# Queries by one f32 matmul instead of three bf16 parts, one-hots in f32 with two chunks interleaved, and a ring of three for the block sums

## The reference

```python
q = (X @ Wq)[src]                 # 64 wide
k = (X @ Wk)[dst]
e = jnp.tanh(q + k)
scores = e @ Wphi
exp_scores = jnp.exp(scores - jnp.max(scores))
denom = jax.ops.segment_sum(exp_scores, src, num_segments=N)
alpha = exp_scores / (denom[src] + 1e-09)
msg = alpha[:, None] * ((X @ Wy_w + Wy_b)[dst] + e @ We)
out = jax.ops.segment_sum(msg, src, num_segments=N)
x = layernorm(x + out)
```

## Time and profile before

| | |
|---|---|
| median of three runs | 5431.57 us (5428.85 to 5432.63) |
| the profiled execution | 5425.74 us, of which the span of its instructions is 5424.0 us |
| PE matmul | 3511.2 us busy, 65% of the span |
| PE weight load | 2746.3 us, 51% |
| DVE | 4216.0 us, 78% |
| ACT | 3684.6 us, 68% |
| POOL | 3537.4 us, 65% |
| mean granted clock of TensorE | 0.779 of full |

### The profile page before, as it was taken

One profiled execution on the slowest core, in us unless ns is written; L12 is line 12 of the kernel. 1 busy time (PEld: TensorE's weight loads), 2 busy tenths in 40 slices (PEclk: granted clock), 3 DMA queues, 4 the chain that ended last, 5 costly groups with the idle time before them and its releaser, 6 DMA issues. The chain is left out here.

```text
span 5424.0 us, 91419 instructions
## 1 busy us (share of the span) xinstructions
PE 3511.2 (65%) x19333; PEld 2746.3 (51%) x19333; DVE 4216.0 (78%) x9852; ACT 3684.6 (68%) x14197; POOL 3537.4 (65%) x3559
## 2 busy tenths in 40 slices
PE   7799999955555665555655555556655555556557
PEld 7566566644444444444444444444544444444446
DVE  7699999977777777777777777777777777777776
ACT  3699999966666666666666666666666666666667
POOL 1034434357777777777777777777777777777771
PEclk9899999977777767777777777776677777777778
DMA  3200000023333333333333333333333333333334
GB/s 89 73 5 5 5 5 5 5 71 106 106 106 102 106 106 107 103 106 106 106 103 107 106 105 103 106 107 105 104 106 107 106 103 106 106 105 102 106 98 110
DMA packets 284190, 478.09 MB, mean 88 GB/s; under 512 B 94226, under 2 KB 203892, under 8 KB 283385
## 3 DMA queue, kind: packets, MB, share of 16 engines
q0 software_dynamic: 165184, 324.30, 23.0%
q1 hardware_dynamic: 100662, 142.95, 7.8%
q10 hardware_dynamic: 17794, 4.91, 0.4%
HBM read 456.43 MB, written 20.60 MB: 88 GB/s over the span
## 5 line engine op out<-in xcount | busy, mean ns | idle before, releaser
L1112 POOL DMA_INDIRECT gathered<-table,dst_rows x3276 | 3151.2, 962 | 1008.9 <-issue 992.1
L1146 PE MATMUL bank<-gathered,weighted_onehots 128*128 128x193 f32 x6592 | 1913.4, 455 | 1458.6 <-DVE block_sums L1235 1450.4
L1146 PEld LDWEIGHTS bank<-gathered,weighted_onehots 128*128 128x128 f32 x6592 | 1582.1, 267 | 1661.9 <-issue 997.4
L1235 DVE TENSOR_TENSOR block_sums<-block_sums,bank 128x193 f32 x3296 | 1166.8, 354 | 541.1 <-issue 166.0
L1198 DVE TENSOR_REDUCE gathered<-bank 128x128 f32<-128x384 f32 x1648 | 840.5, 552 | 446.0 <-DMA gathered<-table,dst_rows 435.0
L1157 ACT ACTIVATE gathered<-gathered 128x256 f32<-128x256 f32 x824 | 346.5, 421 | 1202.8 <-DVE gathered L1202 1202.8
L1167 ACT ACTIVATE weighted_onehots<-src_distances,score_less_shift 128x128 f32<-128x128 bf16 x3296 | 1052.4, 390 | 26.9
L1175 ACT ACTIVATE src_distances<-row_to,src_in_block 128x128 bf16<-128x128 f32 x3296 | 1039.6, 386 | 0.0
L822 ACT ACTIVATE places_past_far<-bank,stat 128x98 bf16<-128x98 f32 x2727 | 889.2, 1237 | 18.8 <-PE bank L847 18.8
L822 ACT ACTIVATION_READ_ACCUMULATOR places_past_far<-bank,stat 128x1 f32 x2727 | 887.9, 1097 | 0.0
L1135 PE MATMUL bank<-q_parts,src_onehots_T 128*128 x3296 | 614.7, 317 | 272.6 <-DVE gathered L1202 231.2
(11 more groups left out here) (190 smaller groups left out, 2272.5 us busy)
## 6 DMA issues: line engine op xcount, KB each, us to landing
src_in_block_rows<-src_in_block_list SPq DMA_DIRECT2D x206, 512.0 KB
gathered<-table,dst_rows POOLq DMA_INDIRECT x3276
gathered<-table SPq DMA_DIRECT2D x2560, 0.8 KB
table<-in_x SPq DMA_DIRECT2D x4, 1562.5 KB
x_in<-in_x SPq DMA_DIRECT2D x24, 256.0 KB, 2.9
x_again<-in_x SPq DMA_DIRECT2D x48, 128.0 KB, 2.3
out<-out_rows SPq DMA_DIRECT2D x48, 128.0 KB, 1.9
sorted_list<-sorted_groups,unit_destinations POOLq DMA_INDIRECT x248
```

The lines of the kernel that those rows point to most:

```text
L1112: e.indirect_dma_start(slot[:, r, j, 0:ROW], None, table, bass.IndirectOffsetOnAxis(ap=gidx[:, t:t + 1].bitcast(u32), axis=0)).then_inc(ga ...
L1146: made = e.matmul(SM[q % 2 * 2 + j // 2][:, o:o + SUMS], ohw[:, q % 3, j, :], slot[:, r, j, A:SLOT], start=True, stop=True)
L1235: e.tensor_tensor(sums[:, bass.ds(b, SUMS)], sums[:, bass.ds(b, SUMS)], SM[q % 2 * 2 + j // 2][:, o:o + SUMS], ALU.add).then_inc(accumulat ...
```

## The change

The queries are kept as one f32 array. The query matmul of a tile is one f32 matmul with 64 columns, and the four tiles of a step go to one bank. The one-hots for it are written in f32, into an array in which the two chunks alternate element by element, so that both the writing VectorE instruction and the weight load step over every second f32 element. The two reductions of line 1198 go; the addition of the key reads the queries from PSUM. The banks that come free make a ring of three steps for the products, and the sums are added one step later (s-5). The plan loses the operations that made the parts, and two steps of its loop.

```diff
-        q3 = sb(ctx, "q_parts", [PARTS, NB * 3 * A], bf16)
+        q32 = sb(ctx, "queries", [PARTS, NB * A], f32)
...
-        XSTEPS = NQ + XR + 2
+        XSTEPS = NQ + XR
...
-                    e.activation(q3v[:, b0:b0 + n, 0, :], kst[:, k % XR, 0:n, A:2 * A], ACT.Copy).then_inc(q0_made, 1)
-                k = i - (XR + 1)
-                if 0 <= k < NQ:
-                    b0, n, _ = q_split(k)
-                    e.wait_ge(rest_made, k + 1)
-                    e.activation(q3v[:, b0:b0 + n, 1, :], rest[:, k % 2, 0:n, :], ACT.Copy).then_inc(q1_made, 1)
+                    e.activation(q32v[:, b0:b0 + n, :], kst[:, k % XR, 0:n, A:2 * A], ACT.Copy).then_inc(queries_kept, 1)
...
-                    e.tensor_tensor(rest[:, k % 2, 0:n, :], kst[:, k % XR, 0:n, A:2 * A], q3v[:, b0:b0 + n, 0, :],
-                                    ALU.subtract).then_inc(rest_made, 1)
...
-                    e.tensor_tensor(q3v[:, b0:b0 + n, 2, :], rest[:, k % 2, 0:n, :], q3v[:, b0:b0 + n, 1, :], ALU.subtract).then_inc(q2_made, 1)
...
-        ohT = sb(lists, "src_onehots_T", [PARTS, 2, CHUNK * PARTS], bf16)
+        ohT = sb(lists, "src_onehots_T", [PARTS, CHUNK * PARTS, 2], f32)
...
-        QK, SM = [[bank[0], bank[1]], [bank[2], bank[3]]], [bank[4], bank[5], bank[6], bank[7]]
+        QK, SM = [bank[0], bank[1]], [[bank[2 + 2 * i], bank[3 + 2 * i]] for i in range(3)]
...
-        TAIL = 5
+        TAIL = 6
...
-                        made = e.matmul(QK[q % 2][j // 2][:, j % 2 * 3 * A:(j % 2 + 1) * 3 * A], ohT[:, c % 2, o:o + PARTS], q3[:, bass.ds(b, 3 * A)],
+                        made = e.matmul(QK[q % 2][:, j * A:(j + 1) * A], ohT[:, o:o + PARTS, c % 2], q32[:, bass.ds(b, A)],
                                         start=True, stop=True)
...
-                    if q >= 2:
-                        e.wait_ge(accumulated, (q - 1) * QUAD)
+                    if q >= 3:
+                        e.wait_ge(accumulated, (q - 2) * QUAD)
...
-                        made = e.matmul(SM[q % 2 * 2 + j // 2][:, o:o + SUMS], ohw[:, q % 3, j, :], slot[:, r, j, A:SLOT], start=True, stop=True)
+                        made = e.matmul(SM[q % 3][j // 2][:, o:o + SUMS], ohw[:, q % 3, j, :], slot[:, r, j, A:SLOT], start=True, stop=True)
...
-            e.tensor_scalar(ohT[:, c % 2, :], lob[:, c % LOB, :], part0[:, :], None, ALU.is_equal).then_inc(onehots_T_made, 1)
+            e.tensor_scalar(ohT[:, :, c % 2], lob[:, c % LOB, :], part0[:, :], None, ALU.is_equal).then_inc(onehots_T_made, 1)
...
-                    for h in range(2):
-                        made = e.tensor_reduce(slot[:, r, 2 * h:2 * h + 2, ROW:ROW + A], QK[q % 2][h][:, 0:6 * A].rearrange("p (j s f) -> p j f s", s=3, f=A),
-                                               AX.X, ALU.add)
-                    made.then_inc(query_summed, 1)
-                    e.wait_ge(query_summed, q + 1)
-                    e.tensor_tensor(slot[:, r, :, ROW:ROW + A], slot[:, r, :, ROW:ROW + A], slot[:, r, :, 0:A], ALU.add).then_inc(added_qk, 1)
+                    e.tensor_tensor(slot[:, r, :, ROW:ROW + A], QK[q % 2][:, 0:QUAD * A].rearrange("p (j f) -> p j f", f=A),
+                                    slot[:, r, :, 0:A], ALU.add).then_inc(added_qk, 1)
...
-                q = step - 4
+                q = step - 5
...
-                        e.tensor_tensor(sums[:, bass.ds(b, SUMS)], sums[:, bass.ds(b, SUMS)], SM[q % 2 * 2 + j // 2][:, o:o + SUMS],
+                        e.tensor_tensor(sums[:, bass.ds(b, SUMS)], sums[:, bass.ds(b, SUMS)], SM[q % 3][j // 2][:, o:o + SUMS],
                                         ALU.add).then_inc(accumulated, 1)
```

More of the change, by code:

```diff
@@ L110, in gnn_program @@
         used = sb(ctx, "tiles_used", [1, 1], i32)
-        q3 = sb(ctx, "q_parts", [PARTS, NB * 3 * A], bf16)
+        q32 = sb(ctx, "queries", [PARTS, NB * A], f32)
         bmap = sb(ctx, "tile_blocks", [PARTS, 2, MAPC], i32)
-        q3v = q3[:, :].rearrange("p (b s f) -> p b s f", s=3, f=A)
+        q32v = q32[:, :].rearrange("p (b f) -> p b f", f=A)
         fences = {k: sem(f"fence_{k}") for k in ENGINES}
@@ L164, in gnn_program @@
         x_padded, x_turned, xT_made, kq_made, kst_made = sem("x_padded"), sem("x_turned"), sem("xT_made"), sem("kq_made"), sem("kst_made")
-        q0_made, rest_made, q1_made, q2_made = sem("q0_made"), sem("rest_made"), sem("q1_made"), sem("q2_made")
+        queries_kept = sem("queries_kept")
         hots_made, tiles_counted, tiles_out = sem("hots_made"), sem("tiles_counted"), sem("tiles_out")
@@ L415, in gnn_program @@
         kst = sb(plan, "k_and_q", [PARTS, XR, GB, 2 * A], f32)
-        rest = sb(plan, "q_rest", [PARTS, 2, GB, A], f32)
         tot_row = sb(plan, "block_tiles_int", [PARTS, NB], i32)
@@ L489, in scalar_plan @@
                         e.wait_ge(k_stored[k % XR], x_loads(k - XR))
-                        e.wait_ge(rest_made, k - XR + 1)
-                        e.wait_ge(q0_made, k - XR + 1)
+                        e.wait_ge(queries_kept, k - XR + 1)
                     e.activation(kst[:, k % XR, 0:n, :], kq, ACT.Copy).then_inc(kst_made, 1)
@@ L642, in vector_plan @@
             line.after()
-            line.did(e.tensor_scalar(bmap[:, 0, :], bmf[:, :], float(3 * A), None, ALU.mult))
+            line.did(e.tensor_scalar(bmap[:, 0, :], bmf[:, :], float(A), None, ALU.mult))
             line.did(e.tensor_scalar(bmap[:, 1, :], bmf[:, :], float(SUMS), None, ALU.mult))
@@ L1008, in gnn_program @@
         distances_made, onehots_T_made = sem("src_distances_made"), sem("src_onehots_T_made")
-        query_summed = sem("query_summed")
         queried, added_qk, tanh_made = sem("queried"), sem("added_qk"), sem("tanh_made")
@@ L1016, in gnn_program @@
         leave = {k: sem(f"pass_next_{k}") for k in ENGINES if k != "sync"}
-        pass_sems = [*gathered, *rows_by_sync, *lows_loaded, sums_cleared, distances_made, onehots_T_made, query_summed, queried, added_qk, tanh_made,
+        pass_sems = [*gathered, *rows_by_sync, *lows_loaded, sums_cleared, distances_made, onehots_T_made, queried, added_qk, tanh_made,
                      times_phi, scored, scores_shifted, weighted, totalled, accumulated, row_max, core_max, shift_made, *steps_over.values()]
-        QK, SM = [[bank[0], bank[1]], [bank[2], bank[3]]], [bank[4], bank[5], bank[6], bank[7]]
+        QK, SM = [bank[0], bank[1]], [[bank[2 + 2 * i], bank[3 + 2 * i]] for i in range(3)]
         CLEAR = NB * SUMS * 4 // 9
@@ L1133, in tensor_steps @@
                         o = t % CHUNK * PARTS
-                        b = e.snap(regs[t % CHUNK], min_val=0, max_val=(NB - 1) * 3 * A)
-                        made = e.matmul(QK[q % 2][j // 2][:, j % 2 * 3 * A:(j % 2 + 1) * 3 * A], ohT[:, c % 2, o:o + PARTS], q3[:, bass.ds(b, 3 * A)],
+                        b = e.snap(regs[t % CHUNK], min_val=0, max_val=(NB - 1) * A)
+                        made = e.matmul(QK[q % 2][:, j * A:(j + 1) * A], ohT[:, o:o + PARTS, c % 2], q32[:, bass.ds(b, A)],
                                         start=True, stop=True)
```

## The result

The changed kernel takes 5529.05 us (median of four runs, 5526.56 to 5529.73), the kernel before on the same chip 5430.73 us: a ratio of 1.0176, interval 1.016 to 1.0192. It is slower by 1.8%. The forecast was 5537, with 5500 to 5590 for its own case and 5375 to 5590 with the fast rival.

A forecast was written before the change was run, and what follows sets the result against it. GpSimd's gathers were taken to bound the kernel. Terms +127 - 14 - 8 = +105 us on the profiled 5425.74 gave 5531, and 5.8 us for the median made 5537 us, +1.9%; range 5375 to 5590.

The forecast's parts named there:

- its own case: Main part: f32 one-hots at two numbers a cycle still exclude gathers; 5537 us, chance 0.64.
- the fast rival: One-hots' strided store runs at one number a cycle and leaves gathers alone; 5385 us, chance 0.27.
- GpSimd is the bound: Main part: GpSimd's gathers fill it, 3151.2 us busy plus 992.1 us issue, of 4150 us.
- Line 1182 keeps excluding gathers: Main part, one-hots: writing f32 takes 1.29 us and still shuts out GpSimd's gathers.
- The stall: Gathers beside the one-hots lengthen by 0.74 us a chunk, 152 us, 25 there before: +127 us.
- the formulas: Gather lengthening from one-hots' duration L and start s: s + L + 0.12 - 0.95 below s = 0.45, another form above.
- the shift of 0.2: One-hots start about 0.2 us later into a gather; 0.77 us average lengthening by the formulas.
- Addition from PSUM: Key addition reads one operand from PSUM, so fewer gathers are held: -14 us (0 to -23).
- Plan: Plan before the main part: removed copies and two last steps save time, -8 us (0 to -12).
- Query matmul: TensorE, main part: f32 queries take 1.0 to 2.1 us a step, fitting beside the products, so 0.
- The second rival: TensorE becomes the bound with queries and products at 5.3 us a step; 5643 us, chance 0.03.
- the clock argument: TensorE staying at the lower clock when over 90% busy is unlikely; the sort, 92% busy, has 1.00.

The follow-up runs named there:

- last experiment: Changed kernel with tensor_scalar and PSUM-operand one-hots alternating by 36 chunks, ring of two, GpSimd clearing an array each step; 6471.9 us, kernel before 5437.09.
- light gathers: Gathers fetch 64 numbers instead of 192, in the changed kernel, the version with partition number in PSUM, and the kernel before: 6159.15, 6149.05, 6186.31 us.

## Why the prediction was right

*GpSimd is the bound.* Held, before and after, by the waits. The last experiment shows it by a difference in time (25.1 us) that is the difference in the gathers' own duration (25.2 us), though the two kinds of block also differ in VectorE's work and in TensorE's clock.

*Line 1182 keeps excluding gathers when it writes f32.* Held. Of the two ends that I had for the unknown store, two numbers a cycle (1.29 us) came (1.283), and the exclusion with it. The dense layout makes no difference, so the row of line 589 was the near one and that of line 1367 the far one.

*The stall: 0.74 us a chunk, +127 us.* Measured 0.750 and +128. It rests on the phase. I had the one-hots follow the addition of the key by about 1.36 us and they do by 1.33, and most then begin 0.25 to 0.42 us into a gather. Put to the phases as they lie in the changed kernel, with L = 1.283, the formulas give 0.75, so they hold for the longer instruction too. The phases themselves were not shifted one by one: 183 of the 206 are between 0.20 and 0.45, where the shift of 0.2 would have put 128. The average hardly depends on that (0.77 by the shift), and that 0.74 came within 0.01 is in part luck, as my own trials went from 0.65 to 0.88.

*Addition from PSUM, -14 us.* Measured -17. Gathers over 1.0 us away from the one-hots fell from 130 to 38. What is left is the 9 us forecast; what there was is 26 us by the split above, where the prediction had 22.6, hence 17 for 14. That the rest comes from the multiplication by phi is shown by the version with phi in PSUM, where it goes.

*Plan, -8 us.* The destinations are made at 208.17 for 220.26, 12.1 us earlier; 9.5 of it is left at the first gather.

*Query matmul, 0.* Held: 1207.3 us over 824 steps is 1.47 us a step (1.0 to 2.1 forecast), products and queries together 3.76 us of the 5.17 that a step takes, and GpSimd waited for TensorE 1.8 us. The second rival is out. By its wait, that is, and not by the clock argument that I had against it: another run has a stretch of the plan with TensorE 92% busy and a granted clock of 0.50 (last section), so the row of the sort did not carry it.

*VectorE's time, ring of three, tail.* VectorE's saving went into waits; the sums' wait for `totalled` fell from 28.9 to 1.2 us, hidden; the tail is 1.0 us longer (within 1.5).

The terms came to +128 - 17 - 9.5 + 1.0 = +102.5 against the 103.1 of the spans, and against +105 forecast. The 5537 lies 8 us over the 5529: 2 by the terms, and 5.8 that I had added because the profiled execution of the kernel before lay under its median; after the change it lies on it (5529.14).

*The fast rival* (0.27) needed the exclusion to go with the strided f32 store. It did not; but an instruction of the same output that leaves the port alone exists (2.28 us), and its gathers have the 953 ns that this rival wanted. Its time as a whole kernel on a chip of the first kind was not measured. From the rows: 3276 times 996 less 953 ns is 141 us under the span of 5527.1, an estimate of 5386 us, 38 under the span before. It assumes that nothing else becomes the bound, as in the blocks of this form in the last experiment.

## What to carry to other kernels

When an engine that issues transfers is the bound, work removed from another engine is worth little by itself (here VectorE gave up 741 us, and the time rose), and what that engine's remaining instructions do to the issuer can be worth more. Look for the few long instances of the bounding instruction (mean against median), find what lies beside each, and work the new duration through the phases as they lie. A cheaper instruction that takes the shared port can cost more than one almost twice as long that does not.

## What had not been expected

The hold of a gather goes by the placement of operands as sharply as shown: 2.28 us with one operand in PSUM, surplus 0.01 us; the same with both in SBUF, 1.98 us.

Chips differ in when gathers land: the addition of the key, which waits for it, starts 2.8 us after the last gather's start on one kind and about 20 on the other, with the same 0.946 us of the instruction, and the kernel before takes 5431 or about 6160 us. Only bytes were tried, and they are not the reason (264 or 478 MB, 6150 us); the cause stays open. On these chips the loss of 1.8% does not appear: versions of the changed kernel with the same long gathers have ratios of 0.9955 to 0.9972. With light gathers, the first gather starts at 1150.1 after the change and 1181.0 in the kernel before, 30.9 us apart, while first to last start differ by 6.2 us (4883.2 and 4889.3). So there the early part is what is left to see, and nearly all of the 30.9 us is there when the destinations are made (208.7 and 239.5; on the first chip 208.2 and 220.3). The traces show what goes with its being more than the 12.1 us of the first chip. The same 20 us of the plan (start:end, us, busy of PE, PEld, DVE, ACT and POOL with their counts, granted clock, DMA share, GB/s), in the kernel before on the first chip and then in the kernel before with light gathers:

```profile
180.00:200.00 20.00, 17.04 (x193) 15.16 (x192) 12.91 (x41) 14.72 (x32) 0.00 (x0) 1.00 0.60 157
180.00:200.00 20.00, 18.40 (x134) 17.62 (x134) 9.49 (x29) 10.90 (x23) 0.00 (x0) 0.50 0.42 109
```

In the second TensorE has the lower clock from there to the end of the plan, and the matmuls of keys and queries (line 528) take 405 ns on average for 290. With the transposes of line 517 beside it they are busy 70.3 us for 45.0. So some 19 of the 30.9 us (the 12.1 taken off) go with TensorE's clock in that execution, and not with operations that the change took away. Why the clock was low there stays open, and this is the only trace of a kernel before on such a chip. The changed kernel itself was not run on these chips.
